# A four-stage sequence model on one core: the odd half chunks of two feed-forward weights packed into one, a product of high and low halves joined, two biases taken off TensorE

## The reference

```python
    q = heads(x @ q_w.T + q_b);  k = heads(x @ k_w.T + k_b);  v = heads(x @ v_w.T + v_b)   # 16 heads of 16
    qp = elu(q) + 1;  kp = elu(k) + 1
    kv = einsum('bhsd,bhse->bhde', kp, v)
    z = einsum('bhsd,bhd->bhs', qp, kp.sum(axis=2))[..., None]
    x = layernorm(x + (einsum('bhsd,bhde->bhse', qp, kv) / (z + 1e-6)) @ o_w.T + o_b)
    # ternary feed-forward: w1, w2 are (704, 256), w3 is (256, 704)
    quantize(w) = clip(round(w / (mean(abs(w)) + 1e-8)), -1, 1)
    x1 = x @ quantize(w1).T;  x2 = x @ quantize(w2).T
    x = layernorm(x + (sigmoid(x1) * x2) @ quantize(w3).T)
```

## Time and profile before

| | |
|---|---|
| median of 3 runs | 431.73 us (431.62 to 432.14) |
| profiled execution | 434.08 us, its span 432.3 us |
| mean granted TensorE clock | 0.949 |
| busy share of the span | PE 89%, DVE 68%, ACT 48%, POOL 30% |
| laps 2, 3, 4 (with gathers) | 20.67, 20.64, 20.68 us |
| laps 5, 6 (no gathers) | 20.07, 20.00 us |

### The profile page before, as it was taken

The page is one execution under the profiler, slowest core; times in us unless marked ns, Lnnn a source line. Parts: engine busy times, 40 slices in busy tenths (PEclk is TensorE's granted clock), DMA queues, the critical chain, the costliest instruction groups (busy, mean ns, idle before and its releaser), DMA issues.

```text
span 432.3 us, 7368 instructions
## 1 busy us (share of the span) xinstructions
PE 384.6 (89%) x2260; PEld 332.9 (77%) x2260; DVE 294.3 (68%) x789; ACT 205.9 (48%) x419; POOL 129.5 (30%) x226
## 2 busy tenths in 40 slices
PE   3999999999739889999999868999999999999691
PEld 3888888888627677777777657988889889999690
DVE  4787999999982456687453255676868686866532
ACT  3374586558652433345335414554455544636341
POOL 2002256444632430003201167234435240401111
PEclk9999999999867999999999985999999999999977
DMA  6543954211122345733431131102020100000000
GB/s 210 184 172 127 137 207 146 70 37 50 49 76 94 99 153 150 247 98 100 134 111 50 52 94 52 50 0 74 4 72 27 49 27 2 24 2 25 2 26 24
DMA packets 28486, 35.70 MB, mean 83 GB/s; under 512 B 3680, under 2 KB 25632, under 8 KB 28192
## 3 DMA queue, kind: packets, MB, share of 16 engines
q1 hardware_dynamic: 19760, 21.72, 17.3%
q0 software_dynamic: 3072, 8.39, 6.0%
q10 hardware_dynamic: 5616, 5.11, 3.4%
HBM read 22.76 MB, written 12.45 MB: 81 GB/s over the span
## 4 chain that ended last, share of the span: by engine, by line
PE 49%; DVE 33%; issue 7%; ACT 6%; POOL 2%; another core or an unknown queue 1%; DMA 1%; SPq 0%; ACTq 0%; POOLq 0%; DVEq 0%
PE bank L394 20%; PE bank L535 10%; PE bank L556 8%; DVE st L1017 4%; PE bank L662 3%; PE bank L545 2%; PE bank L515 2%; PE bank L404 2%; DVE arena L1079 2%; PE bank L717 2%; DVE arena L1082 2%; DVE arena L1059 1%; DVE fl L1421 1%; DVE arena L1450 1%; DVE arena L1355 1%
## 5 line engine op out<-in xcount | busy, mean ns | idle before, releaser
L394 PE MATMUL bank<-arena 128*128 128x256 f32 (+2 forms) x576 | 120.2, 364 | 9.5 <-ACT arena L792 6.7
L394 PEld LDWEIGHTS bank<-arena 128*128 128x128 f32 x576 | 102.0, 195 | 23.4 <-issue 6.7
L778 ACT ACTIVATE arena<-bank 128x256 f32<-128x256 f32 (+1 forms) x118 | 45.5, 424 | 47.7 <-PE bank L556 26.4
L1538 POOL TENSOR_TENSOR ve<-mv,eps 128x2 f32<-128x2 f32 x32 | 7.0, 219 | 165.9 <-DVE mv L1021 165.9
L535 PE MATMUL bank<-gu,arena 128*128 x156 | 54.9, 476 | 0.0
L556 PE MATMUL bank<-dn,arena 96*128 x156 | 41.0, 385 | 4.6 <-DVE arena L1238 3.5
L783 ACT ACTIVATE arena<-arena,nm,rs 128x256 f32<-128x256 f32 x48 | 26.2, 597 | 38.7 <-POOL nm L1543 38.6
L1604 POOL DMA_INDIRECT arena<-yg,ypos x32 | 31.3, 978 | 39.0 <-DMA yg<-arena 30.6
L1238 DVE COPY arena<-bank 96x256 f32<-96x256 f32 x39 | 16.3, 419 | 39.1 <-PE bank L545 31.6
L556 PEld LDWEIGHTS bank<-dn,arena 96*128 96x128 f32 x156 | 28.7, 190 | 15.1 <-issue 7.0
L1578 POOL DMA_INDIRECT xg<-x,pos x32 | 34.3, 1073 | 14.7 <-issue 7.5
(11 more groups left out here) (207 smaller groups left out, 866.1 us busy)
## 6 DMA issues: line engine op xcount, KB each, us to landing
arena<-xg SPq DMA_DIRECT2D x39, 128.0 KB, 2.1
yg<-arena ACTq DMA_DIRECT2D x39, 128.0 KB
arena<-in_xT SPq DMA_DIRECT2D x8, 256.0 KB
x<-in_x SPq DMA_DIRECT2D x8, 256.0 KB, 4.4
out<-arena SPq DMA_DIRECT2D x8, 256.0 KB
gu<-in_w_gate SPq DMA_DIRECT2D x1, 1408.0 KB, 8.2
gu<-in_w_up SPq DMA_DIRECT2D x1, 1408.0 KB, 6.9
dn<-in_w_down SPq DMA_DIRECT2D x11, 128.0 KB, 6.0
```

Source lines behind the costliest of these rows:

```text
L394: last = pe.matmul(dst, l, r, start=i == 0, stop=i == len(pairs) - 1)
L778: return act.activation(dst, src, ACT.Copy)
```

## The change

1. Row chunk 5 (64 rows) of w2 moves into the unused half of chunk 5 of `w1q`: one product of 128 rows gives both halves, x1 in partitions 0 to 63 and x2 in 64 to 127. `w2q` has five chunks left, so `ternary(b, 2)` has 12 matmuls in place of 16. `tanh_half`, `gate_times`, `f_high` and `f_low` of pair 2 become two instructions each, one for chunk 4 (128 x 256) and one for chunk 5 (64 x 256), which reads and writes other partitions.
2. The low half of chunk 5 is put into partitions 0 to 63 of `fh`, its high half in 64 to 127, and the 64 rows of w3 stand twice in `w3q`, so that one matmul does both: `ternary_out(b, 2)` has 6 matmuls in place of 8. The sum of |w3| is taken in two instructions.
3. The value bias is left out of `keys_values` (2 matmuls); `mask_kv` adds it to the masked `kv`, as value_bias times the column of `kv` that sums kp.
4. The output bias is left out of `attention_out` (2 matmuls); GpSimd adds it to x2 in `bias_residual`, after x2 was transposed and before `attention_residual` reads it.

```diff
                 for w, dst in zip((w1q, w2q), ternary_banks(b, p)):
                     for i in range(2):
+                        if w is w2q and 2 * p + i == NF - 1:
+                            continue
...
-                        for q, l in enumerate((fh, fl)):
+                        for q, l in enumerate((fh, fl) if f < NF - 1 else (fh,)):
...
-                        last = product(halves(dst)[:, t, :], [(pick[:, :], biases[:, cols])] + [
+                        last = product(halves(dst)[:, t, :], ([(pick[:, :], biases[:, :])] if j == 0 else []) + [
...
-                pe.wait_ge(kvm_ok, s + 1)
+                pe.wait_ge(kvm_ok, 2 * (s + 1))
...
-                    last = product(halves(BANK_O)[:, t, :], [(pick[:, :], biases[:, 2 * C:3 * C])] + [
-                        (anT[:, k, chunk(t)], wo3[:, k, :]) for k in range(KC)])
+                    last = product(halves(BANK_O)[:, t, :], [(anT[:, k, chunk(t)], wo3[:, k, :]) for k in range(KC)])
...
+                    act.activation(fb[n % 2][:, 0, :], src[:, 0, :], ACT.Tanh, scale=0.5)
+                    last = act.activation(fb[n % 2][LEFT:P, 1, :], src[0:LEFT, 1, :], ACT.Tanh, scale=0.5)
...
+                    copy(fh[:, n % 2, 0, :], fb[n % 2][:, 0, :])
+                    last = copy(fh[LEFT:P, n % 2, 1, :], fb[n % 2][LEFT:P, 1, :])
...
-                    dve.tensor_reduce(wsum[:, 2:3], raw3[:, :, :], mybir.AxisListType.XY, ALU.add,
-                                      apply_absolute_value=True).then_inc(wsum_ok, 1)
+                    for rows_of, n in ((slice(0, LEFT), NF), (slice(LEFT, P), NF - 1)):
+                        last = dve.tensor_reduce(wsum[rows_of, 2:3], raw3[rows_of, 0:n, :], mybir.AxisListType.XY, ALU.add,
+                                                 apply_absolute_value=True)
+                    last.then_inc(wsum_ok, 1)
...
+                    dve.scalar_tensor_tensor(f[:, 0, :], f[:, 0, :], 1.0, second[:, 0, :], ALU.add, ALU.mult)
+                    last = dve.scalar_tensor_tensor(f[LEFT:P, 1, :], f[LEFT:P, 1, :], 1.0, first[LEFT:P, 1, :],
+                                                    ALU.add, ALU.mult)
...
+                    dve.tensor_tensor(fl[:, n % 2, 0, :], fb[n % 2][:, 0, :], fh[:, n % 2, 0, :].bitcast(F32),
+                                      ALU.subtract)
+                    last = dve.tensor_tensor(fh[0:LEFT, n % 2, 1, :], fb[n % 2][LEFT:P, 1, :],
+                                             fh[LEFT:P, n % 2, 1, :].bitcast(F32), ALU.subtract)
...
-                dve.tensor_tensor(kvm[:, :, :], halves(BANK_KV)[:, :, 0:KVW], msk[:, :, :], ALU.mult).then_inc(kvm_ok, 1)
+                kv = halves(BANK_KV)
+                if s == 0:
+                    dve.wait_ge(bias_ok, 2)
+                dve.tensor_tensor(kvm[:, :, :], kv[:, :, 0:KVW], msk[:, :, :], ALU.mult).then_inc(kvm_ok, 1)
+                dve.wait_ge(kvm_ok, 2 * s + 1)
+                for k in range(KC):
+                    one = P * (KC - 1 - k)
+                    last = dve.scalar_tensor_tensor(kvm[:, k, :], value_bias[:, k, :], kv[:, k, one:one + 1],
+                                                    kvm[:, k, :], ALU.mult, ALU.add)
+                last.then_inc(kvm_ok, 1)
...
             def attention_residual(s):
                 dve.wait_ge(o3_ok, s + 1)
+                dve.wait_ge(x2b_ok, s + 1)
...
+            def bias_residual(b):
+                pool.wait_ge(x2Tp_ok, b + 1)
+                if b == 0:
+                    pool.wait_ge(in_bias, 48)
+                pool.tensor_tensor(x2[b % 2][:, :, :], x2[b % 2][:, :, :],
+                                   out_bias[:, :].unsqueeze(1).broadcast_to([P, NT, C]), ALU.add).then_inc(x2b_ok, 1)
+
             for s in range(B + 2):
+                if s < B:
+                    bias_residual(s)
                 if s >= 2:
                     deviation(3, s - 1)
```

More of the change, by code:

```diff
@@ L23 @@
 NPAIR = NF // 2
+LEFT = HID % P
 HEAD = 16
@@ L104, in build @@
         pick = sb("pick", [P, P], F32R)
-        biases = sb("biases", [P, 3 * C], F32R)
-        bias_hi = sb("bias_hi", [P, 3 * C], F32R)
+        biases = sb("biases", [P, C], F32R)
+        bias_hi = sb("bias_hi", [P, C], F32R)
+        out_bias = sb("out_bias", [P, C])
+        value_bias = sb("value_bias", [P, KC, KVW])
         wdec = sb("wdec", [P, KC])
@@ L227, in build @@
         qtmp = then(NF, C)
-        bias_raw = then(3 * C)
+        bias_raw = then(2 * C)
+        place[0] += C
         yy = [then(NT, 2, C) for _ in range(2)]
@@ L894, in prepare @@
                     act.wait_ge(in_bias, 48)
-                    copy(bias_hi[:, :], bias_raw[:, :])
-                    copy(biases[0:64, :], bias_raw[0:64, :]).then_inc(bias_hi_ok, 1)
+                    copy(bias_hi[:, :], bias_raw[:, 0:C])
+                    copy(biases[0:64, :], bias_raw[0:64, 0:C]).then_inc(bias_hi_ok, 1)
             copy_x1T(B - 3)
@@ L944, in f_high @@
                 past(act, w3_ok, n - 1)
-                copy(fh[:, n % 2, :, :], fb[n % 2][:, :, :]).then_inc(fh_ok, 1)
+                if p < NPAIR - 1:
+                    last = copy(fh[:, n % 2, :, :], fb[n % 2][:, :, :])
+                else:
+                    copy(fh[:, n % 2, 0, :], fb[n % 2][:, 0, :])
+                    last = copy(fh[LEFT:P, n % 2, 1, :], fb[n % 2][LEFT:P, 1, :])
+                last.then_inc(fh_ok, 1)
             def x3_high(b):
@@ L1320, in prepare @@
                     dve.wait_ge(low_ok, i - 11)
[L1321 to L1324, removed]
+                    whole = HID - LEFT
+                    parts = ([(w1q[:, k, 0:HID], slice(0, HID))] if j == 0 else
+                             [(w2q[:, k, :], slice(0, whole)), (w1q[:, k, HID:], slice(whole, HID))])
+                    for dst, cols in parts:
+                        last = dve.scalar_tensor_tensor(dst, raw12[:, j, k, cols], thr[:, 0, j:j + 1], below[:, cols],
+                                                        ALU.is_gt, ALU.subtract)
+                    last.then_inc(quant_ok, 1)
                 if 16 <= i < 21:
@@ L1414, in gate_times @@
                 dve.wait_ge(th_ok, n + 1)
-                dve.scalar_tensor_tensor(fb[n % 2][:, :, :], fb[n % 2][:, :, :], 1.0, halves(ternary_banks(b, p)[1]),
-                                         ALU.add, ALU.mult).then_inc(fx_ok, 1)
+                first, second = (halves(i) for i in ternary_banks(b, p))
+                f = fb[n % 2]
+                if p < NPAIR - 1:
+                    last = dve.scalar_tensor_tensor(f[:, :, :], f[:, :, :], 1.0, second, ALU.add, ALU.mult)
+                else:
+                    dve.scalar_tensor_tensor(f[:, 0, :], f[:, 0, :], 1.0, second[:, 0, :], ALU.add, ALU.mult)
+                    last = dve.scalar_tensor_tensor(f[LEFT:P, 1, :], f[LEFT:P, 1, :], 1.0, first[LEFT:P, 1, :],
+                                                    ALU.add, ALU.mult)
+                last.then_inc(fx_ok, 1)
             def f_low(b, p):
```

47 lines of the change are left out of this document (30 added, 17 removed).

## The result

| | before | after |
|---|---|---|
| median | 431.68 us (431.04 to 432.14, 4 runs) | 442.63 us (440.91 to 443.74, 4 runs) |
| profiled execution, its span | 434.08, 432.3 | 442.02, 440.3 |
| laps 2 to 4, laps 5 and 6 | 20.67, 20.04 | 21.28, 21.27 |

The changed kernel is slower: 1.0254 of the time before, with a 95% interval of 1.0225 to 1.0283. I forecast 437.1 us, with a range of 431.3 to 439.0.

A forecast was written before the change was run, and what follows sets the result against it. A chain of waits over VectorE to `attend`, then mainly TensorE, bounds each lap, though TensorE is 89% busy. Stage C +4.6 and stage B +0.8 give +5.4: span 432.3 to 437.7, median 437.1 us, range 431.3 to 439.0.

The forecast's parts named there:

- The hold: `combined` on VectorE, laps 2 to 6: locked out by GpSimd's bias addition, +1.16 us a lap (0 to 1.3).
- `mask_kv`, +0.66: VectorE ahead of `attend`: two more instructions and a wait, hidden by nothing, +0.66 us a lap (0.45 to 0.95).
- First part: Lap from the seam (first matmul of `ternary_out(b, 2)`) to `attend`: -0.24 + 1.16 + 0.66 = +1.58 us.
- Second part: Lap from `attend` to the next seam: `f_low` starts earlier, splits cost some back, -0.56 us (-0.90 to -0.35).
- The gathers: Laps 2 to 4: the wait behind the last gather should go, -0.40 us in three laps (0 to -0.5).
- Laps 0 and 1: Start of stage C: `mask_kv` and GpSimd costs, less gains from matmuls at half clock and other terms, together +0.5 us.
- Laps 7 and 8: End of stage C: lap 7 sums to 0; lap 8 has splits +0.41 less two matmuls; +0.2 us.
- Stage B: Splitting the sum of |w3| delays a copy, then `down` and all tiles behind: +0.8 us (0 to 1.2).
- The median, -2.35: Step from profiled execution to median: before's median lies 2.35 us under its 434.08, taken off for the changed kernel too.
- No hold: Rival: GpSimd's addition and `combined` run side by side, +0.1 in all, 431.8 us; chance 0.15.
- TensorE decides: Rival: VectorE's additions fall into idle time, all ten matmuls count, -9, 422.7 us; chance 0.07 with milder forms.
- The hold costs more: Rival: `combined` held twice or ScalarE held by a later `deviation`, up to 0.9 more in five laps, 441 us; chance 0.1.

The follow-up runs named there:

- e1: Changed kernel with GpSimd's output-bias addition moved behind the deviation of x2, ahead of the gather; 433.46 us, 1.0159 of before.
- e6: Changed kernel with GpSimd's addition in batches 1 to 7 replaced by a memset that reads no SBUF; 435.58 us, one run.
- e2: Changed kernel with the value bias again a matmul and `mask_kv` again one instruction; 432.40 us, 1.0148 of before.
- e12: Kernel before with pair 2 handed on chunk by chunk and `attention_residual` behind `f_low(b, 2)`, no packing, no bias moved; 420.07 us, 0.9869 of before.
- e9: e8 with pair 2 handed on chunk by chunk and `attention_residual` behind `f_low(b, 2)`; 420.52 us, 0.9817 of before.
- e0: The kernel before once more, no edit, on another chip than the first result; 425.76 us, 0.9998 of before.
- e3: Changed kernel with the two instructions of the sum of |w3| behind tiles 8 and 9 instead of both behind 8; 438.51 us, 1.0292 of before.
- e4: The changed kernel once more, no edit; 442.80 us, 1.0251 of before.
- e5: Changed kernel with 16 unused matmuls filling TensorE's wait in lap 7; 441.22 us, 1.0232 of before.
- e11: Kernel before with 12 unused matmuls filling its TensorE wait in lap 7; 428.42 us, 1.0000 of before.
- third group: e8, e9, e11 and one other kernel, run on one chip with the kernel before, whose median there was 428.28 us.
- second group: e4, e5, e6 and one other kernel, run on one chip with the kernel before, whose median there was 431.86 us.
- e8: Changed kernel with both biases back on TensorE, packing kept, sum of |w3| in two portions; 428.23 us, 0.9995 of before.
- the kernels by chunk: Kernels like e9 and e12 that hand pair 2, or all pairs, on chunk by chunk; medians 418.64 to 420.52 us.

## Why the prediction was wrong, step by step

*The hold, +1.16.* Right in place and cause; measured 1.08 to 1.10 (e1; 1.55 for 0.45). The Trainium skill (SBUF — State Buffer, "SBUF: two separate sides") gives the lock only against a GpSimd operation that reads SBUF; the trace agrees: L1381 took 0.45 beside the memset of e6.

*`mask_kv`, +0.66.* Measured 0.68 (e2).

*First part, +1.58.* 330.30 to 341.65 is 11.35, so +1.51: right, `attend` 11.4 after the seam as forecast.

*Second part, -0.56.* It took 9.94 against 10.23, so -0.29, just beyond the end that I gave (-0.35). The failed terms are those of the splits on ScalarE: 0.05 each for tanh and `f_high`. I had them from copies out of PSUM. From the start of tanh to that of the gate it is now 0.81 (before 343.55 to 344.18, 0.63), from `f_high` to `f_low` 0.88 (before 0.63, the length of `f_high`): +0.18 and +0.25. VectorE's two, +0.17 and +0.18, were as forecast. That a pair on different partitions is dearer can now be read: two gates of 256 columns took 0.75 in e12, both on partition 0, and 0.87 from 356.42 to 357.29 in e9, where the second starts at partition 64 (and has 64 partitions); 0.76 and 0.87 for `f_low`. The changed kernel, with no wait inside the pairs, took 0.85 and 0.86. The Trainium skill (VectorE: DVE Perf Modes, "Two Vector instructions with no wait between them") says that an instruction which starts in another quadrant than the last starts only when all before it have finished; the trace agrees, at a price of 0.10 to 0.12 for the pair.

*The gathers, -0.40 in three laps.* Right for the trace that I had: laps 2 to 4 went up by 0.6 (forecast 0.62), laps 5 and 6 by 1.2 (1.02). But the wait is the chip's: e0 does not have it, and there all five laps are 1.2 longer.

*Laps 0 and 1, +0.5.* Measured 1.0. I had put the hold in laps 2 to 6 alone, but `combined(1)` in lap 0 was held too, by the addition that stood there behind the eight gathers:

```profile
257.96 1.98 DVE L1381 SCALAR_TENSOR_TENSOR arena<-arena,topw,x 128x256 f32<-128x256 f32 x1
```

```profile
258.38 1.27 POOL L1675 TENSOR_TENSOR arena<-arena,out_bias 128x512 f32<-128x512 f32 x1
```

VectorE's instruction starts 0.42 ahead of the addition and is held all the same; e3, e4, e5 and e6 show it too (1.98 to 2.07). That the missing 0.5 is this hold is likely but not shown: e1 took the hold away and put a wait of 3.01 in its place.

*Laps 7 and 8, +0.2.* Measured 1.0 in the profiles. Lap 7 is 1.36 longer. Its first part, seam to `attend`, is 10.14 for 9.36: `mask_kv` and nothing against it, as the 0.24 of the seam were under another wait. The -0.90 + 0.46 of the second came to -0.02, because of the splits. The rest is the seam's end at half clock: 1.61 from the seam to `block_out`, where the seams before have 1.0.

*Stage B, +0.8.* 1.0; right in mechanism. The second sum was 1.48 (I had 1.47).

*The median, -2.35.* This is the largest failed step. I took off the whole distance between the profiled execution and the median, as if the changed kernel's would have it too. The profiled execution was one in which TensorE fell to half clock from 409.0 to 415.9 us, behind a wait of 1.85; this costs 2.0 (14.61 against 12.61 in e0, the same program, which waits 1.84 and keeps the full clock). The means of the granted clock say that it is not the usual case. A stretch of 6.9 us at half clock is 0.008 of the mean of a span of 432. The profiled execution, with 0.949, has half clock at the end of stage A, in laps 0 and 1 (13.7 us), here, and at the kernel's end. e11's profile, with 0.965, has none here and 6.8 us in laps 0 and 1. All 23 executions of the third group have 0.964 or more, which leaves no room for a stretch here unless laps 0 and 1 had less of it than in any profile of before; the 0.956 to 0.964 of the 17 in the second group leave it open for some. The changed kernel waits 2.58 in that place, and both of its profiles (and those of e1 to e3 and e6 to e8) have the half clock there; e5, with the wait filled, has not. The medians differ by 10.95 where the profiled executions differ by 7.94: 2.4 of the 3.0 between is before's own distance, 0.6 the changed kernel's. So the clock, which I had named as what would make the forecast wrong, did, at the end of lap 7 and not before `attend`. That before has the full clock there in most runs is inferred from the mean clocks and from e11, where filling the wait gained nothing, all on other chips than the first; e0's is the only profile of before that shows it. On the first chip it is not shown.

The 5.5 us between 437.1 and 442.6 are 2.5 of the sum (0.6 up to 167.9 in stage B, most likely chance, 0.2 in the rest of it, 0.5 in laps 0 and 1, 0.4 in laps 2 to 6 and 0.8 in laps 7 and 8) and 3.0 of the step to the median. In laps 2 to 6 both causes of loss were right, and the term of the splits was too small; in lap 7 the splits and the clock, in lap 0 the second hold, were left out.

*Rivals.* "No hold" fell with L1381. "TensorE decides" fell with the waits of 0.9; only in the kernels by chunk does TensorE fill the lap. "The hold costs more" did not occur: L1384 and the others kept 0.48.

Open is why one chip waits 0.6 for the last gather's end and another, with the same rows on GpSimd, does not.

## What to carry to other kernels

Work taken off the busiest engine is worth nothing where that engine waits at the end of the stretch; look first at what the halves of a split operation make wait, and hand each on by itself (here 0.7 us a lap, together with one residual moved back, against 0.46 for the six matmuls of the packing). A GpSimd operation that reads SBUF belongs where VectorE has no instruction with two SBUF inputs, which a few lines further down was free. Before going from a profiled span to a median, ask what made that one execution longer, and whether the changed kernel is exposed to it always.

## What the runs showed that I had not expected

- In the profiles of e4 and e5, sixteen matmuls that compute nothing took 1.57 us off the stretch behind them: with its wait of 2.6 us filled down to 0.68, TensorE kept its full clock (2.4 GHz), and without them it fell to 1.2 GHz.
- A split in two on ScalarE (128 x 512 to 128 x 256 and 64 x 256 in other partitions) cost 0.18 to 0.25 us, as much as on VectorE; out of PSUM, in the same partitions, the pair of tanh took 0.66 (e12, one row of the trace for both) and 0.78 in different ones; the pair of roundings took 0.72 in e12 and 0.85 in the changed kernel.
- One program differs by 1.4% from chip to chip (426.0 to 431.9), part of it in a wait that one chip has and another has not, and a ratio to it moves with the chip.
